# Attention and a routed expert layer: a tile's two row scatters moved half a step apart, the input loads put behind another event, and the ring of rows made longer

## What is computed

```python
x = x + tanh(g_xattn[0]) * xattn(layernorm(x), ctx, ctx)
x = x + tanh(g_ffn[0]) * ffn(layernorm(x))
...
# xattn: 16 heads of width 8; rotary turn of keys and values; softmax over 64 keys; output product and bias
qp, kp, vp = q @ Wq.T, rope(k @ Wk.T), rope(v @ Wv.T)
weights = softmax(einsum('bhqd,bhkd->bhqk', qh, kh) / sqrt(8))
...
# ffn: 8 experts, the two best of each token, weighted by a softmax of their two gate logits
top_k_weights, top_k_indices = top_k(x @ gate_kernel, 2)
expert(x) = (silu(x @ w0) * (x @ w1)) @ wo        # 128 -> 256 -> 128
```

## Time and profile before

| | |
|---|---|
| executions without a recording | 549.70, 551.46 and 552.86 us; median 551.46 |
| recorded execution, span from the first to the last instruction | 665.6 us |
| PE matmuls busy in it | 561.5 us, 84% |
| ACT / DVE / POOL busy | 431.8 / 393.9 / 384.0 us |
| first to last attention tile's input turned on PE | 4.3 to 359.1 us |
| granted TensorE clock, mean of the span | 0.971 |

### The profile page before, as it was taken

How to read it: one execution, slowest core, us unless ns; L and a number is a source line. 1 busy time by engine, 2 the same in 40 slices (tenths; PEclk the granted TensorE clock), 3 DMA queues, 4 the chain that set the end, 5 groups by cost and what they waited for, 6 DMA issues and landing times.

```text
span 665.6 us, 21070 instructions
## 1 busy us (share of the span) xinstructions
PE 561.5 (84%) x6123; PEld 468.0 (70%) x6124; DVE 393.9 (59%) x1418; ACT 431.8 (65%) x1090; POOL 384.0 (58%) x524
## 2 busy tenths in 40 slices
PE   8998898998989899899898779787778978888960
PEld 6886676776767677677776668676677868877860
DVE  6797787777778677677778643372133323223663
ACT  4897787887787788788777735344244546556540
POOL 3347756576575666657566466575545555545651
PEclk9999999999999999999999899897899999999995
DMA  3801111111111111111112112233222222225996
GB/s 91 240 20 57 42 42 52 36 55 40 48 44 36 56 40 48 48 33 58 41 55 63 33 50 73 64 98 101 85 64 80 77 74 76 76 68 174 270 272 206
DMA packets 64242, 52.98 MB, mean 80 GB/s; under 512 B 8607, under 2 KB 60064, under 8 KB 64176
## 3 DMA queue, kind: packets, MB, share of 16 engines
q1 hardware_dynamic: 46560, 30.79, 16.5%
q0 software_dynamic: 8448, 16.93, 7.7%
q10 hardware_dynamic: 9168, 4.46, 2.3%
HBM read 29.44 MB, written 23.22 MB: 79 GB/s over the span
## 4 chain that ended last, share of the span: by engine, by line
PE 51%; another core or an unknown queue 15%; issue 10%; ACT 8%; DVE 6%; ACTq 3%; DMA 2%; DVEq 2%; POOL 1%; SPq 1%; POOLq 0%
PE psK L583 10%; PE psH L603 8%; PE psH L483 5%; PE psH L489 4%; PE psG L498 4%; PE psH L498 3%; PE psK L471 3%; ACT wcur L757 3%; PE psO L619 2%; ACTq L319 2%; ACT ys L771 2%; PE psK L619 2%; ACT hs L764 2%; PE psO L518 2%
## 5 line engine op out<-in xcount | busy, mean ns | idle before, releaser
L1251 POOL DMA_INDIRECT results<-ys,zin x136 | 136.1, 1001 | 106.5 <-ACT ys L771 68.3
L603 PE MATMUL psH<-zT,wcur 128*128 128x128 f32 (+1 forms) x760 | 139.1, 333 | 20.1 <-ACT wcur L757 15.2
L1178 POOL DMA_INDIRECT lists<-zp,dest x128 | 129.6, 1012 | 34.8 <-issue 31.1
L603 PEld LDWEIGHTS psH<-zT,wcur 128*128 128x128 f32 x760 | 112.8, 195 | 34.4 <-ACT wcur L757 20.1
L1083 DVE TENSOR_TENSOR hm<-psH,hs 128x512 f32<-128x512 f32 x68 | 47.0, 692 | 121.0 <-remote 45.7
L977 DVE TENSOR_REDUCE mx<-psH 128x8 fp32r<-128x512 f32 x128 | 82.5, 686 | 43.4 <-PE psH L483 23.6
L696 ACT ACTIVATE ex<-psH,rs 128x512 f32<-128x512 f32 x128 | 86.8, 688 | 23.9 <-PE psH L489 16.3
L583 PEld LDWEIGHTS psK<-v,pT 128*64 128x64 f32 x2048 | 69.6, 137 | 37.1 <-issue 36.3
L583 PE MATMUL psK<-v,pT 128*64 128x64 f32 x2048 | 81.1, 226 | 9.0 <-issue 8.6
L757 ACT COPY wcur<-w 128x512 f32 x95 | 56.1, 619 | 15.2 <-issue 14.2
L747 ACT COPY v<-kvr 64x64 f32<-64x64 f32 x256 | 63.7, 249 | 2.2
(11 more groups left out here) (176 smaller groups left out, 1140.5 us busy)
## 6 DMA issues: line engine op xcount, KB each, us to landing
yy<-results SPq DMA_DIRECT2D x16, 512.0 KB
zin<-lists SPq DMA_DIRECT2D x41, 130.0 KB
out_dram<-x ACTq DMA_DIRECT2D x16, 256.0 KB
xring<-in_x_dram SPq DMA_DIRECT2D x31, 128.0 KB
cring<-in_ctx_dram SPq DMA_DIRECT2D x31, 128.0 KB
zin<-lists SPq DMA_DIRECT2D x54, 65.0 KB
results<-ys,zin POOLq DMA_INDIRECT x136
w<-in_L_ffn_w_kernel_dram SPq DMA_DIRECT2D x2, 1024.0 KB, 7.1
```

The costliest lines, as they stand in the source:

```text
L603: last = pe.matmul(bank[t.buf(2)][:, k * ET + c.start:k * ET + c.stop], wcur[:, t.buf(2), h, a, k * P:(k + 1) * P], zT[:, t.buf(2), c], st ...
L1178: nc.gpsimd.indirect_dma_start(lists, bass.IndirectOffsetOnAxis(ap=dest[:, t.buf(4), j:j + 1], axis=0), zp[:, t.buf(4), j, :], None).then_ ...
L1251: nc.gpsimd.indirect_dma_start(results, bass.IndirectOffsetOnAxis(ap=zin[:, t.buf(8), h, D:D + 1].bitcast(U32), axis=0), ys[:, t.buf(8), h ...
```

## The change

It has three parts.

1. **Scatters.** The scatter of a tile is made a step later (for tile s-6 in step s, not s-5) and in two pieces. The first waits for `kv_ps` of tile s+5, that is, for PE's keys and values in the same step s; it stands ahead of the powers. The second waits for `q_sb` of tile s+4, that is, for ACT's copy of the queries in step s; it stands behind the powers and the product `gaps`. The copy of the token numbers (`tokens`) and the first count sum (`counted`), once in four tiles, come behind it, and the other count sums behind those.
2. **Ring.** `zp`, `dest` and `row_out` are rings of 8 tiles instead of 4, so the writers wait for the scatters of the tile eight before.
3. **Loads.** In the loop SP no longer waits for `x1` and for POOL's variance of tile t-7; it waits for the buffers, and then for the turn of the keys of tile t-4 (`kT_ps`), which PE makes in its step t-7.

The steps at which DVE's and ACT's hardware loops begin are 10 and 14 instead of 7 and 11.

```diff
-ATT_DVE = Pipeline(NT, behind=2, ahead=5, unroll=8, steady=7, turns=5)
-ATT_ACT = Pipeline(NT, behind=6, ahead=1, unroll=8, steady=11, turns=5)
-ATT_POOL = Pipeline(NT, behind=5, ahead=5, unroll=8, steady=10, turns=5)
+ATT_DVE = Pipeline(NT, behind=2, ahead=5, unroll=8, steady=10, turns=5)
+ATT_ACT = Pipeline(NT, behind=6, ahead=1, unroll=8, steady=14, turns=5)
+ATT_POOL = Pipeline(NT, behind=6, ahead=5, unroll=8, steady=10, turns=5)
...
-        zp = sb("zp", [P, 4, 2, ROW])
+        zp = sb("zp", [P, 8, 2, ROW])
...
+                def between_scatters(t):
+                    wait_for(sp, kT_ps, t, back=4)
...
                     for u in (0, 2):
-                        wait_for(sp, x1_done, Tile(4, turn, u - 7))
-                        carry(sp)
                         load_ready(Tile(4, turn, u))
-                        scattered(Tile(4, turn, u - 7))
+                        carry(sp)
+                        between_scatters(Tile(4, turn, u))
                         load(Tile(4, turn, u))
...
-                    wait_slot(act, row_out, t, 32, back=4)
+                    wait_slot(act, row_out, t, 32, back=8)
...
-                    if (t := ATT_POOL.at(s, -2)) and t.buf(4) == 3:
-                        tokens(t)
-                    if not static(s, NT - 1):
-                        powers(ATT_POOL.at(s, 0), ATT_POOL.at(s, 3))
-                    if (t := ATT_POOL.at(s, -2)) and t.buf(4) == 3:
-                        counted(t)
-                    if t := ATT_POOL.at(s, -5):
-                        scatter(t, range(2))
+                    if t := ATT_POOL.at(s, -6):
+                        if u := ATT_POOL.at(s, 5):
+                            wait_for(pool, kv_ps, u)
+                        scatter(t, (0,))
                     if static(s, NT):
                         powers(ATT_POOL.at(s, -1), None)
+                    elif not static(s, NT - 1):
+                        powers(ATT_POOL.at(s, 0), ATT_POOL.at(s, 3))
...
+                    if t := ATT_POOL.at(s, -6):
+                        if u := ATT_POOL.at(s, 4):
+                            wait_for(pool, q_sb, u)
+                        scatter(t, (1,))
+                    if (t := ATT_POOL.at(s, -2)) and t.buf(4) == 3 and not static(s, NT + 1):
+                        tokens(t)
+                        counted(t)
```

More of the change, by code:

```diff
@@ L193, in flamingo_block @@
         hit = sb("hit", [P, 4, 2, E])
-        dest = sb("dest", [P, 4, 2], U32)
+        dest = sb("dest", [P, 8, 2], U32)
         tokid = sb("tokid", [P, NT, 2], U32)
@@ L228, in flamingo_block @@
         tok_done, route_ready, pad_ready, spare_out = sem("tok_done"), sem("route_ready"), sem("pad_ready"), sem("spare_out")
-        row_out = [sem(f"row_out{i}") for i in range(4)]
+        row_out = [sem(f"row_out{i}") for i in range(8)]
         pad = sb("pad", [P, 2, ROW])
@@ L371, in _ @@
                     for u in (0, 2):
-                        wait_for(sp, x1_done, Tile(4, turn, u - 7))
+                        load_ready(Tile(4, turn, u))
                         carry(sp)
-                        load_ready(Tile(4, turn, u))
-                        scattered(Tile(4, turn, u - 7))
+                        between_scatters(Tile(4, turn, u))
                         load(Tile(4, turn, u))
@@ L404, in _ @@
                 for n in row_out:
-                    sp.wait_ge(n, 32 * (EARLY // 4))
+                    sp.wait_ge(n, 32 * (EARLY // 8))
                 for t in (0, 1):
@@ L427, in _ @@
                 for n in row_out:
-                    sp.wait_ge(n, 32 * (NT // 4))
+                    sp.wait_ge(n, 32 * (NT // 8))
                 sp.wait_ge(filled, 16 * E)
@@ L688, in normalised @@
                     wait_for(act, nm_done, t + (0 if t.buf(2) else 1))
-                    wait_slot(act, row_out, t, 32, back=4)
-                    nc.scalar.activation(zp[:, t.buf(4), :, 0:D], one(x1, t).unsqueeze(1).broadcast_to([P, 2, D]), ACT.Identity,
+                    wait_slot(act, row_out, t, 32, back=8)
+                    nc.scalar.activation(zp[:, t.buf(8), :, 0:D], one(x1, t).unsqueeze(1).broadcast_to([P, 2, D]), ACT.Identity,
                                          scale=rs[:, t.buf(4) // 2, 2 + t.buf(2):3 + t.buf(2)],
@@ L965, in row_weights @@
                     for i in (3, 2, 1, 0):
-                        wait_slot(dve, row_out, t + -i, 32, back=4)
-                    nc.vector.tensor_scalar(zp[:, :, 0, D + 1], egap[:, :], -0.5, 0.5, ALU.mult, ALU.add).then_inc(weight_done, 2)
-                    nc.vector.tensor_scalar(zp[:, :, 1, D + 1], egap[:, :], 0.5, 0.5, ALU.mult, ALU.add).then_inc(weight_done, 2)
+                        wait_slot(dve, row_out, t + -i, 32, back=8)
+                    g = slice(t.buf(8) - 3, t.buf(8) + 1)
+                    nc.vector.tensor_scalar(zp[:, g, 0, D + 1], egap[:, :], -0.5, 0.5, ALU.mult, ALU.add).then_inc(weight_done, 2)
+                    nc.vector.tensor_scalar(zp[:, g, 1, D + 1], egap[:, :], 0.5, 0.5, ALU.mult, ALU.add).then_inc(weight_done, 2)
                 def destinations(t):
@@ L1178, in scatter @@
                         nc.gpsimd.indirect_dma_start(
-                            lists, bass.IndirectOffsetOnAxis(ap=dest[:, t.buf(4), j:j + 1], axis=0),
-                            zp[:, t.buf(4), j, :], None).then_inc(row_out[t.buf(4)], 16)
+                            lists, bass.IndirectOffsetOnAxis(ap=dest[:, t.buf(8), j:j + 1], axis=0),
+                            zp[:, t.buf(8), j, :], None).then_inc(row_out[t.buf(8)], 16)
                 def tokens(t):
@@ L1241, in attention_step @@
                                                 rs[:, :, 2:4], ALU.mult).then_inc(gaps_done, 4)
+                    if t := ATT_POOL.at(s, -6):
[5 more added lines that the diff above has]
+                        counted(t)
+                    if (t := ATT_POOL.at(s, -1)) and t.buf(4) == 3:
+                        wait_for(pool, chosen_done, t)
+                        for i in range(3):
+                            wait_for(pool, before_done, t, back=4 - i)
+                            nc.gpsimd.tensor_tensor(before[:, i + 1, :], before[:, i, :], chosen[:, i, :], ALU.add).then_inc(before_done, 1)
                 pool.wait_ge(zero_ready, 3)
-                ATT_POOL.run(pool, attention_step, until=NT)
+                ATT_POOL.run(pool, attention_step, until=NT + 1)
                 def experts_step(s):
```

11 lines of the change are left out of this document (3 added, 8 removed).

## The result

| | before | changed |
|---|---|---|
| executions without a recording, median (lowest to highest) | 550.48 us (548.72 to 552.86) | 553.42 us (551.10 to 554.39) |
| changed over before | | **1.0042 [1.0023, 1.0060]** |
| recorded execution, span | 549.1 us | 549.4 us |

The time lies inside the range that was given and within the 0.5% called no change, but on the other side of the gain of 2 us that was forecast, and the interval excludes a gain. That it fell into the forecast's own range of 548.7 to 554 us was luck: the gain was absent, and a loss of about the same size stood at a place that the sum had put at 0. The changed kernel's recorded execution was one of its fastest: the spans of its nine executions have a median of 551.7 us. One recorded span doesn't tell 2 us; the ratios do.

The account below looks back on a forecast made before the run. The prediction took timed executions to run almost at PE's pace in both stages. Scatters gave -2 us and all other terms 0: 551.46 - 2 = 549.5 us, with 538 to 558 us as the range for 8 in 10.

Parts of the forecast that it names:

- What bounds the kernel: Both stages, attention and experts: timed executions run almost at PE's pace; the recording's 51 and 63 us are not paid.
- Between nothing and some 8 us: Whole kernel: what timed executions still pay for holds, perhaps more if matmuls are drawn out in the recording.
- Scatters: Attention: parting the two scatters takes back a little over half of 3.6 us: -2 us, ends 0 and -12.
- The waits on POOL: Attention's odd steps: powers 0.45 us later with 0.6 us of cover left, and `kvr` in time: cost 0.
- Ring: Rings of 8 tiles: the same instructions on larger buffers, covering the later scatters: 0.
- Loads: SP's loads in attention: out some 2 to 3 us earlier, beside the first scatter, covered by the ring: 0.
- The ends: Tile 47's second scatter 4.8 us later, hidden by SP's 10.7 us table wait; more plain DVE and ACT steps: 0.
- The signs of being wrong: Timed median falls 5 us or more, or rises with PE waiting for exponentials or ACT for POOL's `rs`.
- Rival 1: Holds beside scatters are in timed executions too: change takes 5 to 12 us, about 544 us; chance 0.39.
- Rival 2: Powers behind the first scatter in odd steps make the exponentials late: slower, 559 us with 0.3 us over; chance 0.19.
- Rival 3: Odd steps' second scatter pairs with the next tile's first: gain 1 us, 550.5 us; inside the forecast's 0.42.
- the forecast's case: Timed median: a gain of 0 to 2.7 us or a loss as small, rival 3 included; chance 0.42.

Follow-up runs that it names:

- the second recording: The kernel before, without an edit, recorded once more: recorded span 549.1 us, 549.80 us without a recording, ratio 0.9998.
- the tail mended: The changed kernel, but from step 60 POOL's list is that of before, with one tile caught up: 1.0002 over before.
- the earlier trace: The recording of the unchanged kernel that the prediction was made from: span 665.6 us, median without a recording 551.46 us.
- spreading the eight: Scatters of tiles 60 to 63 at every fourth expert step instead of every second: 0.9957 on before, 1.0005 on the change.
- 0.9957: Ratio of the kernel before with only the eight scatters of tiles 60 to 63 spread to every fourth expert step.
- 1.0005: Ratio to before of the changed kernel with the eight scatters of tiles 60 to 63 spread to every fourth expert step.
- The two kernels with late pairs: Last attention scatters in pairs, one step late: on the changed kernel 1.0002, on before with rings of 8 alone 1.0003.

## Why the prediction was wrong, by its own steps

**What bounds the kernel: right.** The timed executions run almost at PE's pace, and the recorded 51 and 63 us of holds were not paid: the second recording spans 549.1 us and PE is busy 268.3 of 270 us. "Between nothing and some 8 us" left over was nearer to nothing in attention: 1.7 us of PE idle in those 270. The second recording has no wait of DVE over 0.3 us from 100 to 300 us. The Trainium skill's page "SBUF — State Buffer", section "Who interferes with whom", says that a reduction on VectorE never contends with GpSimd and that PE never waits on anyone for a port of the SBUF. This recording agrees; only the first one spoke against it.

***Scatters*, -2 us: the size failed.** The term took a little over half of 3.6 us of holds that the second recording doesn't have. With the tail mended, parting inside attention measures 1.0002 [0.9988, 1.0015]: no gain is seen, which is the term's end at 0.

***The waits on POOL*, 0: right.** ACT waits for POOL nowhere from 100 to 300 us. POOL's wait for DVE fell from 21.7 us to none and came back as 16.2 us of waits for the two events.

***Ring* and *Loads*, 0: right**, by 0.9996 and 1.0008. That SP no longer waits for `x1` shows in its waits from 100 to 350 us of the changed kernel, against the earlier trace rows (there 180.0 us for `x1`; 129.1 in the second recording of before):

```profile
SPq L122 <- PE psX L531: 84.8, 20, 4.7
SPq L408 <- DVE table L887: 11.5, 1, 11.5
```

***The ends*, 0: the step that failed.** It followed tile 47, whose rows the experts' first load needs, and was right there (the first expert tile at 321.4 us against 321.2, and SP waits 11.5 us for the table). It didn't follow what else the later and parted scatters stand in front of on POOL: the scatters of the results. The first of these comes 1.8 us later, measured from the first expert tile, so the buffer of tile 0 comes free later, and with it the load of tile 8, for which PE then waits: 1.6 us of PE's time from 340 to 360 us. By the ratio the loss is 0.42%, or 2.3 us; the recordings place 1.6 of it, and where the rest goes they don't show. The lack of slack among the experts (two scatters of about 1.0 us with 0.30 between, 2.6 us a tile, against PE's 2.84, and the eight of tiles 60 to 63 on top) is a cost of the kernel before as well, and spreading the eight leaves the change's loss as it was. Which part of the delay is the late step and which the parting stays open.

The signs of being wrong that the prediction named don't point there: ACT waited for `rs` once in attention, 0.5 us between 60 and 100 us, and PE is as busy there as before.

**Rival 1** (holds in the timed executions) is refuted by the second recording. What spoke for it was read too strongly: in the earlier trace rows PE's run stops at 245.60 + 1.09 = 246.69 us, 0.14 us after the scatter's end at 245.59 + 0.96 = 246.55, and not during it. **Rival 2** had the sign and POOL's order right, but another place: the powers stayed in time for the exponentials. **Rival 3** came out within the forecast's case but can't be told from it, since there was no hold to keep or lose.

## What to carry to other kernels

When work on a queue is reordered in a steady loop, follow it to the end of the loop: the loop may have slack for the new order while the first work of the next stage on that queue has none. There the old order, pairs back to back and the small sums behind them, can be kept for the last steps alone. And when two changes are tried together, the sum is compared with each of them alone: only beside 0.9957 does 1.0005 show that the loss was still there. And a recording that is far longer than the timed runs is recorded again before anything is built on what it shows.

## What the runs showed of the hardware that I had not expected

The same program was recorded at 665.6 and at 549.1 us. In the first, DVE and PE stood still beside scatters; in the second they didn't. Why that recording differed was not tried.

A scatter that follows a scatter, and waits for no event, mostly starts after 0.30 us of idle. One that follows a sum on POOL started after 0.17 us behind 25 of the sums `kvr` in the second recording of before, and after 0.62 to 0.73 us, there and in the change, from tile 56's first scatter to the first result. No row says what makes the difference.

In front of tile 56's second scatter POOL stood idle for about 2 us, and the trace names nothing that it waited for. The two kernels with late pairs lack that time, 1.8 us of it, which is about what makes up for the lateness in them. This stays open.
